# Graph 0's x and layer outputs transposed by TensorE instead of DMA in a two-layer graph attention kernel, with the prologue's jobs laid anew

## The reference

```python
for k in range(2):                         # the L layers
    q = x @ Wq[k].T + bq[k]; kk = x @ Wk[k].T + bk[k]
    scores = where(rel_edges == 0, -1e10, q @ kk.T / sqrt(128))
    attn = where(mask, 0.0, softmax(scores))
    x = layer_norm(x + (attn @ x) @ Wc[k].T, ln_g[k], ln_b[k])
# the H layer, 8 heads
q, k, v = x @ Wq + bq, x @ Wk + bk, x @ Wv + bv
h = softmax(where(adj == 0, -inf, q @ k.T / sqrt(32))) @ v
return layer_norm(h @ Wo + bo + x) * gamma + beta
```

## Time and profile before

| | us |
|---|---|
| median of 3 runs | 1213.55 (1213.24 to 1213.66) |
| the profiled execution | 1213.54 |
| its span, first to last instruction | 1211.8 |
| PE busy / DVE / ACT / POOL | 1155.4 / 989.3 / 923.2 / 538.9 |

### The profile page before, as it was taken

One profiled execution on the slowest core, in us unless ns is written; L12 is line 12 of the kernel. 1 busy time (PEld: TensorE's weight loads), 2 busy tenths in 40 slices (PEclk: granted clock), 3 DMA queues, 4 the chain that ended last, 5 costly groups with the idle time before them and its releaser, 6 DMA issues.

```text
span 1211.8 us, 28408 instructions
## 1 busy us (share of the span) xinstructions
PE 1155.4 (95%) x9572; PEld 840.7 (69%) x9572; DVE 989.3 (82%) x2680; ACT 923.2 (76%) x2112; POOL 538.9 (44%) x400
## 2 busy tenths in 40 slices
PE   5977999999999999999999999999999999999796
PEld 2754677777777777777777777777777777777463
DVE  4676789888888988888898888889888888988676
ACT  3235887878878787887878788787878888787774
POOL 1452344453464345346434534644453464444330
PEclk9799999999999999999999999999999999999999
DMA  8116161442615243251514325161442617132311
GB/s 242 36 36 153 23 176 36 124 90 71 153 36 167 45 122 88 67 161 36 172 39 123 89 81 146 36 177 34 125 91 78 145 37 179 32 76 79 95 33 36
DMA packets 170687, 114.06 MB, mean 94 GB/s; under 512 B 107184, under 2 KB 152240, under 8 KB 170544
## 3 DMA queue, kind: packets, MB, share of 16 engines
q1 hardware_dynamic: 168384, 104.37, 33.9%
q0 software_dynamic: 2160, 7.87, 1.9%
HBM read 61.87 MB, written 25.17 MB: 72 GB/s over the span
## 4 chain that ended last, share of the span: by engine, by line
PE 74%; DVE 11%; ACT 7%; issue 5%; DMA 2%; POOL 1%; DVEq 0%; POOLq 0%; SPq 0%; ACTq 0%
PE ps_j L793 32%; PE ps_t L806 18%; PE ps_j L910 9%; PE ps_s L779 6%; PE ps_s L785 6%; ACT probs L970 3%; ACT pt_l L976 2%; DVE some_l L1203 2%; DVE masked_s L1066 2%; DVE y_l L1217 2%; DMA xt<-ys 1%; PE ps_j L918 1%; DVE xw L1196 1%; DVE stats_L L1086 1%; DVE pt_l L1101 1%
## 5 line engine op out<-in xcount | busy, mean ns | idle before, releaser
L1066 DVE CUSTOM_DVE_ANT_0 masked_s<-ps_s,mask 128x512 f32<-128x512 f32 x640 | 424.4, 680 | 16.3 <-PE ps_s L785 14.5
L970 ACT ACTIVATE probs<-masked_s,nm_h 128x512 f32<-128x512 f32 x512 | 367.2, 718 | 88.6 <-DVE nm_h L1066 82.3
L806 PE MATMUL ps_t<-ident,probs 128*128 128x128 f32 x2560 | 391.4, 276 | 11.7 <-ACT pt_h L976 6.0
L806 PEld LDWEIGHTS ps_t<-ident,probs 128*128 128x128 f32 x2560 | 305.2, 142 | 93.9 <-issue 31.1
L976 ACT ACTIVATE pt_h<-ps_t 128x512 f32<-128x512 f32 x404 | 237.7, 588 | 64.5 <-PE ps_t L806 61.7
L785 PE MATMUL ps_s<-stack 128*128 128x512 f16 x512 | 194.7, 381 | 4.3 <-DVE nm_h L1066 3.8
L793 PE MATMUL ps_j<-xw,pt_l 128*128 128x256 f16 x1536 | 189.4, 275 | 0.0
L793 PEld LDWEIGHTS ps_j<-xw,pt_l 128*128 128x128 f16 x1536 | 151.4, 99 | 31.1 <-issue 0.5
L608 POOL TENSOR_TENSOR rstd_L<-var_eps_L,minus_half 128x4 f32<-128x4 f32 x32 | 32.8, 1025 | 264.8 <-DVE var_eps_L L1096 264.8
L910 PE MATMUL ps_j<-pt_h,v 128*32 128x256 f32 x2048 | 123.6, 382 | 2.2 <-DVE pt_h L1073 1.9
L1101 DVE TENSOR_TENSOR pt_l<-ps_t,pt_l 128x512 f16<-128x512 f32 x128 | 88.3, 690 | 37.6 <-ACT pt_l L976 28.4
(11 more groups left out here) (123 smaller groups left out, 1647.6 us busy)
## 6 DMA issues: line engine op xcount, KB each, us to landing
stack<-bounce SPq DMA_DIRECT2D x256, 128.0 KB, 3.1
bounce<-parts SPq DMA_DIRECT2D x64, 256.0 KB, 2.7
adj_t<-adj_dram SPq DMA_DIRECT2D x30, 512.0 KB, 5.4
x<-x_dram SPq DMA_DIRECT2D x16, 512.0 KB, 4.0
out_dram<-y_f POOLq DMA_DIRECT2D x15, 512.0 KB, 3.4
stack<-adj_dram SPq DMA_DIRECT2D x2, 512.0 KB, 5.6
pt_h<-l_wc SPq DMA_DIRECT2D x2, 256.0 KB, 4.3
xt<-ys SPq DMA_TRANSPOSE x32, 4.4
```

Source lines behind the costliest of these rows:

```text
L806: last = pe.transpose(ps_t[r % 2][:, t], probs[:, r, t * P:(t + 1) * P], ident[:])
L970: act.activation(probs[:, r], masked_s[:, r], ACT.Exp, bias=nm[:, n, r:r + 1], scale=-1.0, accum_out=total[:, n, r:r + 1]).then_inc(exps, 1)
L1066: dve.tensor_tensor_reduce(out=masked_s[:, r], in0=ps_s[scores_bank(pos)][:], in1=m[:, r], scale=-scale, scalar=NONE_LEFT, op0=ALU.add, op ...
```

## The change

Graph 0's three inputs (x, and the normalised outputs of both L layers) are transposed by PE in a new job X: four 128x128 fp32 transposes per feature half into a PSUM bank, a copy to fp16 by ACT, the low part by DVE. The DMA turns of graph 0 and POOL's splits for them go; those of the other graphs stay, and their semaphore counts are renumbered (`dma_turn`). B keeps the sums of L layer 1; Z has those of the H layer's q and k, U those of its v. `PROMPT` lists jobs that ACT and DVE take at their own tile. Layer 1's low weights move from tile 3 to tile 7 of the first block, the H weights' high parts from block 1 to the end of block 0, N of graph 1's layer 0 from the end of block 0 into block 1, and N of graph 0's layer 1 into the start of block 2, where X and the first head QK follow it. V, C, U, M and half of AV of graph 1 move into the head block, and DVE takes two of four copies of its tiles instead of one. Weights0 are announced one by one. The raw weights lie in slots 3 and 4 of `pt_h`.

```diff
 PRO_BLOCKS = [
     (3, [("L", 0, 0), ("L", 0, 1)],
-     [("S", None, 0, 0), ("QK", (0, 1), 0, 0), ("XW", (2, 0), 0, 0)],
+     [("X", (0, 1), 0, 0), ("S", None, 0, 0), ("QK", (2, 0), 0, 0), ("XW", (1, 2), 0, 0)],
      [("D", None, 0, 0, (1,)),
-      ("QK", (1, 2), 1, 0, (0, 0)),
+      ("QK", (0, 1), 1, 0, (0, 0)),
       ("M", None, 1, 0, (0,)),
       ("N", None, 0, 0, (4,)),
-      ("AV", (0, 1), 0, 0, (2, 2, 3, 3)),
-      ("AV", (0, 2), 1, 0, (6, 7, 7, 7)),
-      ("XW", (2, 0), 1, 0, (3, 4)),
-      ("B", (1, 2), 0, 0, (5,)),
-      ("W", None, 0, 1, (2, 2)),
-      ("M", None, 1, 1, (0,)),
-      ("N", None, 1, 0, (7,))]),
+      ("AV", (2, 0), 0, 0, (2, 2, 3, 3)),
+      ("X", (1, 0), 0, 1, (7, 7)),
+      ("AV", (2, 1), 1, 0, (6, 7, 7, 7)),
+      ("XW", (1, 2), 1, 0, (3, 4)),
+      ("B", (0, 1), 0, 0, (5,)),
+      ("W", None, 0, 1, (3, 7)),
+      ("W", None, 0, 2, (7, None)),
+      ("M", None, 1, 1, (0,))]),
     (3, [("L", 1, 0)],
-     [("QK", (2, 0), 0, 1), ("XW", (1, 2), 0, 1)],
-     [("W", None, 0, 2, (0, 0)),
-      ("AV", (0, 1), 0, 1, (2, 3, 3, 3)),
-      ("N", None, 0, 1, (3,))]),
+     [("QK", (0, 2), 0, 1), ("XW", (0, 1), 0, 1)],
+     [("Z", (2,), 0, 0, (0,)),
+      ("N", None, 1, 0, (1,)),
+      ("W", None, 0, 2, (None, 1)),
+      ("AV", (0, 1), 0, 1, (2, 3, 3, 3))]),
     (3, [("L", 1, 1)],
-     [("QK", (2, 0), 1, 1), ("XW", (1, 2), 1, 1)],
-     [("C", (0,), 0, 0, (1,)),
-      ("M", None, 2, 0, (1,)),
-      ("QH", (0, 1), 0, 0, (3, 3)),
-      ("QH", (1, 2), 0, 1, (3, 3)),
-      ("V", (1, 2), 0, 0, (3, 3)),
-      ("AV", (1, 2), 1, 1, (3, 3, None, None))]),
+     [("QK", (2, 0), 1, 1), ("N", None, 0, 1), ("XW", (1, 2), 1, 1), ("X", (0, 1), 0, 2), ("QH", (2, 0), 0, 0)],
+     [("QH", (1, 2), 0, 1, (2, 3))]),
     (4, [("H", 0, 0), ("H", 1, 0), ("H", 2, 0)],
      [],
-     [("M", None, 2, 1, (5,))]),
+     [("V", (0, 1), 0, 0, (1, 3)),
+      ("M", None, 2, 0, (3,)),
+      ("M", None, 2, 1, (5,)),
+      ("U", (2,), 0, 0, (4,)),
+      ("C", (0,), 0, 0, (6,)),
+      ("AV", (1, 2), 1, 1, (8, 10, None, None))]),
 ]
+PROMPT = {("QK", 1, 0, 0), ("QK", 1, 0, 1), ("W", 0, 1, 0)}
-PRO_COPIES, TAIL_COPIES = [(3,)] * PRO_SLOTS, [(3,)] * 5 + [(1, 3)] * 8
+PRO_COPIES, TAIL_COPIES = [(3,)] * (PRO_SLOTS - 3) + [(1, 3)] * 3, [(3,)] * 5 + [(1, 3)] * 8
...
             load_x(1)
-            turn_x(0, 0)
             load_adj(0, 0)
...
-            turn_x(0, 1)
             load_x(2)
             turn_x(1, 1)
             load_adj(2, 0)
-            turn_x2(0)
...
-            split_x(0)
             split_x(1)
...
             split_x(2)
+            split_y(0, 1)
             pool.wait_ge(y_ready["L"], 2 * nth(0, 1) + 2)
...
+                if name == "X":
+                    if half == 0:
+                        if l == 0:
+                            pe.wait_ge(x_in, 16)
+                        else:
+                            pe.wait_ge(normed["L"], nth(0, l - 1) + 1)
+                    out_bank = bank(banks[half], before)
+                    for t in range(NT):
+                        last = pe.transpose(out_bank[:, t * P:(t + 1) * P],
+                                            (y_l if l else x0)[:, t, half * P:(half + 1) * P], ident[:])
+                    last.then_inc(x_turned, 1)
...
+                if name == "X":
+                    act.wait_ge(x_turned, 2 * l + half + 1)
+                    act.activation(x_parts(l, half)[0], bank, ACT.Copy).then_inc(x_hi, 1)
...
+                if name == "X":
+                    dve.wait_ge(x_hi, 2 * l + half + 1)
+                    hi, lo = x_parts(l, half)
+                    low_part(lo, bank, hi, x_lo)
```

More of the change, by code:

```diff
@@ L315, in scores_since, with dma_turn, wait_xt, wait_xt2 @@
             return next(d for d in range(1, LOOP_TILES) if scores_bank((pos - d) % LOOP_TILES) == scores_bank(pos))
+        def dma_turn(b, l):
+            return (None, 1)[b] + l if b < 2 else nth(b, l) - 1
+        def wait_xt(eng, b, l):
+            if b == 0:
+                eng.wait_ge(x_lo, 2 * (l + 1))
+            else:
+                eng.wait_ge(xt_in, 16 * dma_turn(b, l))
+        def wait_xt2(eng, b):
+            if b == 0:
+                eng.wait_ge(x_lo, 6)
+            else:
+                eng.wait_ge(xt2_in, 16 * b)
+        def x_parts(l, half):
+            return [xt2[:, a, half] if l == 2 else xt[:, l_buffer(0, l), a, half] for a in range(2)]
         def x_tile(b):
@@ L434, in late_jobs, with prompt @@
             def late_jobs(self, k):
-                got = list(self.jobs.get(k - 1, ()))
-                return got + (list(self.jobs.get(k, ())) if k >= self.n - 1 else [])
+                def prompt(j):
+                    return (j[0], *j[2:5]) in PROMPT
+                got = [j for j in self.jobs.get(k - 1, ()) if not prompt(j)]
+                return got + [j for j in self.jobs.get(k, ()) if k >= self.n - 1 or prompt(j)]
         PART_PAIRS = ((0, 0), (0, 1), (1, 0))
@@ L494, in turn_x @@
                     settle(sp)
-                if not early(L, 1):
-                    sp.wait_ge(xt_in, 16 * L)
+                if dma_turn(b, l) > 1:
+                    sp.wait_ge(xt_in, 16 * (dma_turn(b, l) - 1))
                     settle(sp)
@@ L631, in split_x @@
                 settle(pool)
-                if not early(b, 1):
-                    pool.wait_ge(xt_in, 16 * (nth(b - 1, 0) + 1))
+                if not early(b, 2):
+                    pool.wait_ge(xt_in, 16 * dma_turn(b - 1, 0))
                     settle(pool)
-                split(x_tile(b), xs, xs_hi, None if early(b, 1) else xs_ready, b)
+                split(x_tile(b), xs, xs_hi, xs_ready, b - 1)
             def split_y(b, l):
@@ L641, in split_y @@
                 settle(pool)
[L643 to L648, removed]
+                if b == 0:
+                    return
+                if b > 1:
+                    pool.wait_ge(xt2_in, 16 * (b - 1))
                     settle(pool)
-                else:
-                    pool.wait_ge(xt2_in, 16 * b)
+                if l == 1:
+                    pool.wait_ge(xt_in, 16 * dma_turn(b, 1))
                     settle(pool)
[L653 to L656, removed]
+                split(y_l, ys, ys_hi, ys_ready, dma_turn(b, l) - 1)
             def layer_norm_l0(b, l, dst):
@@ L749, in bank @@
                         pe.wait_ge(bias_ready, 1)
+                    if name == "Z":
+                        pe.wait_ge(head_bias_ready, 1)
+                    if name == "U":
+                        pe.wait_ge(bv_ready, 1)
+                    if name == "X":
+                        pe.wait_ge(x_lo, 2 * l + half + 1)
                     if name == "C":
@@ L810, in job, with shift_through @@
                 L = nth(b, l)
+                def shift_through(sums, n, w, c0, shift_n):
+                    for c in range(DC):
+                        last = pe.matmul(sums[:, n:n + 1], w(c)[:, c0:c0 + P],
+                                         shift_c[:, shift_n, c:c + 1], start=c == 0, stop=c == DC - 1)
+                    return last
+                if name == "X":
+                    if half == 0:
+                        if l == 0:
+                            pe.wait_ge(x_in, 16)
+                        else:
+                            pe.wait_ge(normed["L"], nth(0, l - 1) + 1)
[4 more added lines that the diff above has]
+                    last.then_inc(x_turned, 1)
                 if name == "B":
                     wide, sums = (ps_j[bank][:] for bank in banks)
[L815 to L819, removed]
                     bank(banks[0], before)
@@ L848, in job @@
                 if name == "QK":
-                    pe.wait_ge(xt_in, 16 * (L + 1))
-                    if early(b, 2) and half == 0:
-                        pe.wait_ge(weights_ready, l + 1)
+                    wait_xt(pe, b, l)
+                    if early(b, 2) and l == 0:
+                        pe.wait_ge(weights0_ready, half + 1)
+                    if early(b, 2) and l == 1 and half == 0:
+                        pe.wait_ge(weights_ready, 1)
                     out_bank = bank(banks[half], before)
@@ L1022, in job @@
                     bias = (bq1, bk1)[half]
+                    if early(b, 1):
+                        act.wait_ge(head_bias_ready, 1)
                     act.activation(parts[:, l, 2 * half], bank, ACT.Identity, bias=bias[:, l:l + 1])\
```

75 lines of the change are left out of this document (47 added, 28 removed).

## The result

| | us |
|---|---|
| before, median of 20 runs | 1213.69 (1211.22 to 1216.69) |
| after, median of 20 runs | 1209.72 (1205.73 to 1213.14) |
| after / before, with its 95% interval | 0.9967 (0.996 to 0.9975) |
| after, the profiled execution | 1211.54, its span 1209.7 |
| PE busy / DVE / ACT / POOL | 1153.9 / 1001.0 / 925.9 / 531.9 |

What follows compares the result with a forecast made beforehand. PE idles 32.2 us in the prologue, before the 13th head tile's transposes at 127.78; bringing these forward shortens the kernel equally. They were put 7.9 us ahead, less 4.8 for the clock, 3.1 ahead: 1210.5 us, range 1204.5 to 1215.5.

Steps and rivals of the forecast that it cites:

- step 1: Layer 0's input: PE turns x itself, without POOL and DMA, so the first QK product comes at 8.5, 3.3 us earlier.
- Step 2: Graph 1's QK in layer 0 copied promptly: scores at 23.5, 5.0 us ahead; job B at 38.0, 6.8 ahead.
- Step 3: Job B cut in three: 2.5 us stay, Z takes 2.9, U 2.2 to 2.8; the last AV ends 12.7 us ahead.
- Step 4: Layer 1's low weights queued behind graph 1's AV on DVE: QK at 53.0, 4.6 us behind AV instead of 1.06.
- Step 5: Graph 1's normalising moved into block 1: its layer 1 starts at M3+19.1, not M3+13.1; 6.0 us given back.
- M3: Mark: first score product of graph 0's layer 1, at 68.40 before, predicted at 59.3.
- Step 6: No second turn for layer 1, from graph 1's layer 1 to the first head mask: M4 at 100.6, 12.7 us ahead.
- M4: Mark: first head mask, at 113.31 before, predicted at 100.6.
- Step 7: Head block takes V, AV halves, U and C: 19.3 us from M4 to M5 instead of 14.5; M5 119.9.
- Rival (c): U's narrow products drag the head block to half clock, 5 us more: 1217.1 us in total; chance 0.12.
- Step 8: Clock falls behind PE pauses: three of four places charged 1.6 us each, 4.8 in all; M5 at 124.7, total 1210.5.
- M5: Mark: transposes of the 13th head tile, at 127.78 before, predicted at 119.9, with the clock 124.7.

## Why the prediction was right, point by point

**Steps 1 to 3 held.** The marks up to job B lie within 0.7 us of the forecast. In step 1 QK ran at half rate as assumed, and the turn of graph 1 stayed hidden. Its side sum was too large: the twelve QK products of before took 4.5 us (11.78 to 16.32), not 5.2. Step 2's 3.3 us are shown by taking the line out. Step 3 sized B at 2.5; it took 1.8 (38.64 to 40.39), since 8 narrow products cost 0.12 and not 0.18 each: 0.18 came from a row of which most ran at the low clock (0.50 from 46.5 on).

**Step 4 held.** The pause was 4.43 against 4.6, and its cause the one named. What the prediction did not draw from it: the place was worse than the old one by 3.0 us.

**Step 5 had half of the mechanism and too small a size.** Its M3+19.1 was M3+23.5. N ended at M3+9.8 (+11.1 predicted) and the turn was issued in time. The term that failed is "the 2.7 us of head-weight splits": it was taken from rows of before behind POOL's last operation, which ended there at 75.13, and here POOL was started by the same N. The hint stood in that trace: its first pair, begun at 74.64 beside POOL, took 1.16 us and not 0.87. The splits measured 9.8 us. The term that was named as the bound, turn plus POOL, is real but stands second, as the run with the low parts last shows: M3+17.7.

**Step 6 was right in its sum.** From graph 1's QK to M4 23.3 us passed, 22.2 were forecast (100.6 less 78.4). M4 is late by 7.9: 2.35 from M3, 4.4 from step 5, 1.1 from here.

**Step 7 was too dear.** M4 to M5 took 17.8, not 19.3; 0.6 of that is U, which took 1.6 (116.07 to 117.65) where 2.2 were charged, and no run separates the rest. Rival (c), U dragging the head block to the low clock, did not happen: the granted clock is 1.00 from 105 to 126.29.

**Step 8 had the count and not the prices.** Three of the four places fell to 1.2 GHz, as charged, and the one that did not was the head block. That is how it went in this execution: in the trace with the normalising back, the head block's clock read 0.67 from 97 to 100 us and 0.76 from there to 103, and M4 to M5 took 19.2. Priced from rows of after against the same operations at full clock: the AV quarter and its transposes 1.3; twelve QK products at 2.67 and 1.97 instead of 1.46 each, 1.7; AV quarter 2.74, QK 2.77 and 1.87 instead of 1.46 to 1.48 each, 3.0. That is 6.0 against 4.8. Not all of such a price reaches the total: the run that kept TensorE busy took away the last two, priced 4.7, and gained 4.5 at M4, 3.6 at M5 and 2.5 in the median.

**What made the sum right.** Against the 119.9 without the clock, M5 is 6.4 us late: 2.35 up to M3, 4.4 in step 5, 1.1 in step 6, less 1.5 in step 7. The clock's 6.0 lie within these: 3.0 up to M3, 1.3 in step 5, 1.7 in step 6. So without the clock step 5 was 3.1 late, and the others, 0.65, 0.6 and 1.5 early, gave nearly all of it back. The sum held to 1.6 us in the trace (126.29 against 124.7) while one of its terms, the splits, was wrong by 7: the total alone would not have shown that. That these errors cancel is luck. The median lies another 1.8 under the profiled execution, which no step had. The sign fits the reasons given, the early X, the prompt QK and the short B; of these only the prompt QK was tested alone, and without it nothing measurable is left of the gain. For the early X and the short B there are only the marks (M1 3.05 us earlier; 1.8 us for B in place of 8.1).

## What to carry to other kernels

When a job is moved, look not only at what it waits for and who waits for it, but at what it starts on the other engines, and at what stands beside that work in its new place: 1.37 us of normalising in a late place cost 10 us, because it released 9 us of POOL work beside DVE operations with two SBUF inputs (4.0 us by the run with the low parts last) and sent off the DMA turn 14 us later, which bound next. Put POOL's long operations beside DVE work that reads PSUM and at most one SBUF tile, and a job that waits for a round trip behind the copies for which TensorE waits. Test each part of a bundled change alone: this one held parts worth 3.3 us and parts that cost 10 and 3.

## What was not expected of the hardware

- POOL held DVE operation by operation. A run of six short operations beside five long ones of POOL took 9.8 us, where POOL's five took 9.2, as if one of DVE's were let in between two of POOL's. A 128x4 operation with one SBUF input was held too, for 2.12 us, so the count of inputs alone does not decide. Masks and low parts that read PSUM were not: beside POOL they took 0.63 to 0.69 us, as without it.
- 21 fp32 transposes around X, with no product among them and from 1.56 to 6.5 us, brought the QK products behind them to 1.46 us for six, as 42 fp16 products did (1.46); with X's eight transposes alone it was 2.72. The page "TensorE: Matmul & The Clock Gate" of the Trainium skill, section "Part 4: PE-mode transpose", which the prediction cites, states that transposes do not count for the clock; this run speaks against it. It is one execution, and the level is read from durations: the clock record reads 1.00 there in all three kernels.
- One pause of 2.10 us (ahead of B) was followed by the lower level at about 40.8, and the pause of 2.74 in before was not the earlier trace rows.
